# Spreading a column of maxima to all partitions: one turn of a repeated column in place of ones times a diagonal

## The reference

```python
xn = _layernorm(x)
# graph attention, twice (4 heads of 512, then 1 head of 768)
e = leaky_relu(al_s[src] + al_d[dst], 0.2)
m = segment_max(e, dst)              # one maximum for each node and head
ex = exp(e - m[dst])
alpha = ex / (segment_sum(ex, dst)[dst] + 1e-16)
out = segment_sum(h[src] * alpha, dst)
# keys of the linear attention, 12 heads, 256 features
data_dash = einsum('bhnd,md->bhnm', 64 ** -0.25 * k, proj)
m = max(data_dash)                   # ONE maximum over all nodes, heads and features
k_prime = ratio * (exp(data_dash - diag - m) + EPS)
context = einsum('bhnm,bhnd->bhmd', k_prime, v)
x = x + gnn(xn) + mix(xn)
x = x + ffn(layernorm(x))            # 8 experts, 2 chosen
```

## Time and profile before

| | us |
|---|---|
| median of 3 runs | 3684.7 (3683.17 to 3692.01) |
| the profiled execution, its own time | 3687.61 |
| its span, first to last instruction | 3685.8 |
| TensorE busy (matmul) | 3164.4, 86% |
| VectorE busy | 1971.2, 53% |
| GpSimd busy | 1508.9, 41% |
| mean granted TensorE clock | 0.919 of full speed |

### The profile page before, as it was taken

How to read it: one execution, slowest core, us unless ns; L and a number is a source line. 1 busy time by engine, 2 the same in 40 slices (tenths; PEclk the granted TensorE clock), 3 DMA queues, 4 the chain that set the end, 5 groups by cost and what they waited for, 6 DMA issues and landing times. The chain is left out here.

```text
span 3685.8 us, 64870 instructions
## 1 busy us (share of the span) xinstructions
PE 3164.4 (86%) x22058; PEld 2568.9 (70%) x22059; DVE 1971.2 (53%) x4639; ACT 1122.5 (30%) x2437; POOL 1508.9 (41%) x1496
## 2 busy tenths in 40 slices
PE   5994899999999689999799997799999996689920
PEld 4983677777777468888699997566666663479920
DVE  6753566676666454444422221566666664533357
ACT  1322344444444243333311111333333322223321
POOL 1233677777777300000000000777777761233346
PEclk8997999999999789999899998799999996589965
DMA  5655788888888354444465663999999984557767
GB/s 179 206 175 182 237 267 257 275 259 261 263 267 269 116 179 130 142 142 139 149 79 78 78 78 61 356 327 325 329 332 327 328 302 146 193 173 244 240 224 248
DMA packets 264982, 789.34 MB, mean 214 GB/s; under 512 B 81006, under 2 KB 94033, under 8 KB 257142
## 3 DMA queue, kind: packets, MB, share of 16 engines
q0 software_dynamic: 96640, 416.68, 34.7%
q1 hardware_dynamic: 168054, 369.05, 33.7%
HBM read 679.35 MB, written 167.42 MB: 230 GB/s over the span
## 5 line engine op out<-in xcount | busy, mean ns | idle before, releaser
L923 POOL DMA_INDIRECT k_rows<-tab,k_pick x576 | 598.5, 1039 | 234.8 <-issue 162.1
L2130 POOL DMA_INDIRECT m_rows<-tab,m_e x500 | 491.5, 983 | 200.4 <-issue 134.7
L1383 PE MATMUL k_num<-k_rows,k_wt 128*32 128x384 f32 (+1 forms) x3200 | 282.6, 493 | 12.5 <-ACT k_wt L1015 12.5
L142 PE MATMUL g_prod<-g_w_hi,g_h_h 128*128 128x384 f32 x768 | 258.6, 337 | 0.0
L1559 DVE TENSOR_TENSOR f_a_l<-f_turn,f_a_h 128x384 fp32r<-128x384 f32 x200 | 110.2, 552 | 277.4 <-ACT f_a_h L1531 277.2
L144 PE MATMUL g_prod<-g_w_hi,g_h_l 128*128 128x384 f32 x768 | 256.8, 334 | 0.0
L143 PE MATMUL g_prod<-g_w_lo,g_h_h 128*128 128x384 f32 x768 | 256.6, 334 | 0.0
L142 PE MATMUL f_prod<-f_w_hi,f_a_h 128*128 128x512 f32 x576 | 234.2, 407 | 0.0
L1685 POOL MEMSET g_row<- 128x1 f32 x2 | 0.1, 102 | 561.9 <-POOLq L109 561.9
L144 PE MATMUL f_prod<-f_w_hi,f_a_l 128*128 128x512 f32 x576 | 226.1, 393 | 0.0
L143 PE MATMUL f_prod<-f_w_lo,f_a_h 128*128 128x512 f32 x576 | 224.5, 390 | 0.0
(11 more groups left out here) (366 smaller groups left out, 7820.6 us busy)
## 6 DMA issues: line engine op xcount, KB each, us to landing
agg<-k_outb SPq DMA_DIRECT2D x100, 384.0 KB
f_a_in<-agg SPq DMA_DIRECT2D x100, 384.0 KB, 6.6
h<-f_e SPq DMA_DIRECT2D x25, 1024.0 KB, 4.2
g_h<-h SPq DMA_DIRECT2D x25, 1024.0 KB, 12.2
ys<-e_y SPq DMA_DIRECT2D x56, 384.0 KB, 3.0
tab<-q_xn SPq DMA_DIRECT2D x25, 388.5 KB, 5.9
tab<-g_row SPq DMA_DIRECT2D x25, 385.5 KB, 4.7
m_own<-tab SPq DMA_DIRECT2D x25, 385.5 KB, 9.1
```

Of the source, the lines that this page charges most:

```text
L142: pe.matmul(out, x_hi[k], w_hi[k], start=(k == 0), stop=False)
L923: pool.indirect_dma_start(rows[:, place(u, n), :], None, dram["tab1"], at, bounds_check=bound, oob_is_err=False).then_inc(rows_in[i], 16)
L1383: mm = pe.matmul(num[i][o, 0:n], wt[u % 2][:, v, o], rows[:, place(u, 2 * (half + v) + g), a:a + n], start=(v == 0), stop=(v == 1), tile_p ...
L2130: pool.indirect_dma_start(rows[:, place(h, c) + k, :], None, tab, bass.IndirectOffsetOnAxis(ap=e[h % 4][:, 0, k * SLOTS + c:k * SLOTS + c ...
```

## The change

The column on each partition is no longer put on a diagonal. TensorE's turn (a matmul in transpose mode with the identity) reads the one column 128 times over, with a step of zero along the free dimension: a 128 by 128 tile whose columns are all equal, and whose turn has in each row the whole column. This is done for mcol and rmax in K and for m2 in M. The instructions that made dg and dgm go, with their tiles and semaphores; in M the ones and their memset go too (K keeps ones for another product at its end). The waits of TensorE move from the diagonal to the column, and DVE waits for the spread of the set before ahead of overwriting the column, which it did ahead of overwriting the diagonal. The declarations of tiles and semaphores are left out here.

```diff
@@ -1085,16 +1085,12 @@
 
                 def row_max(t):
                     if t:
-                        dve.wait_ge(dgm_done, t)
+                        dve.wait_ge(top_full, t)
                     dve.tensor_reduce(rmax[:, :], r[:, :], AX.X, ALU.max).then_inc(rmax_done, 1)
-                    dve.wait_ge(rmax_done, t + 1)
-                    if t:
-                        dve.wait_ge(top_full, t)
                     if t == NT - 1:
+                        dve.wait_ge(rmax_done, t + 1)
                         dve.wait_ge(c_in, 16 * (3 if merged else 1))
                         dve.tensor_tensor(rmax[:, :], rmax[:, :], pad[:, :], ALU.add).then_inc(rmax_done, 1)
-                        dve.wait_ge(rmax_done, t + 2)
-                    dve.tensor_scalar(dgm[:, :], keep["ident"][:, :], rmax[:, 0:1], None, ALU.mult).then_inc(dgm_done, 1)
 
                 def running_max(t):
                     dve.wait_ge(top_full, t + 1)
@@ -1211,12 +1207,8 @@
                 def column_max(u):
                     dve.wait_ge(zt_full, u + 1)
                     if u:
-                        dve.wait_ge(dg_done, u)
+                        dve.wait_ge(mrow_full, u)
                     dve.tensor_reduce(mcol[:, :], zbank[:, 0:P], AX.X, ALU.max).then_inc(mcol_done, 1)
-                    dve.wait_ge(mcol_done, u + 1)
-                    if u:
-                        dve.wait_ge(mrow_full, u)
-                    dve.tensor_scalar(dg[:, :], keep["ident"][:, :], mcol[:, 0:1], None, ALU.mult).then_inc(dg_done, 1)
 
                 def shift(u):
                     dve.wait_ge(mrow_full, u + 1)
@@ -1340,12 +1332,12 @@
                     mm.then_inc(cx_full, 1)
 
                 def spread_max(t):
-                    pe.wait_ge(dgm_done, t + 1)
+                    pe.wait_ge(rmax_done, t + 1 if t < NT - 1 else t + 2)
                     if t:
                         pe.wait_ge(acc_done, 4 * t)
                     if merged:
                         pe.wait_ge(pick_done, min(t + 3, NT) if t else 2)
-                    pe.matmul(cx[:, 0:P], ones[:, :], dgm[:, :], start=True, stop=True).then_inc(top_full, 1)
+                    pe.transpose(cx[:, 0:P], rmax[:, 0:1].to_broadcast([P, P]), keep["ident"][:, :]).then_inc(top_full, 1)
 
                 def index_turns(t):
                     pe.wait_ge(ef_done, t + 1)
@@ -1368,8 +1360,8 @@
                     pe.transpose(zbank[:, 0:P], zmax[:, :], keep["ident"][:, :]).then_inc(zt_full, 1)
 
                 def edge_spread(u):
-                    pe.wait_ge(dg_done, u + 1)
-                    pe.matmul(zbank[:, P:2 * P], ones[:, :], dg[:, :], start=True, stop=True).then_inc(mrow_full, 1)
+                    pe.wait_ge(mcol_done, u + 1)
+                    pe.transpose(zbank[:, P:2 * P], mcol[:, 0:1].to_broadcast([P, P]), keep["ident"][:, :]).then_inc(mrow_full, 1)
 
                 def edge_sums(u):
                     pe.wait_ge(wt_done, u + 1)
...
@@ -2113,9 +2105,6 @@
         def _(pool):
             with pool.If(mine(pool)):
                 pool.memset(eps[:, :], MIX_EPS).then_inc(eps_set, 1)
-                if merged:
-                    pool.memset(ones[:, :], 1.0).then_inc(ones_set, 1)
-
                 def gathers(h):
                     pool.wait_ge(e_in[h % 4], 16 * GR * (h // 4 + 1))
                     pool.sem_inc(gather_go, 1)
@@ -2307,12 +2296,9 @@
                     dve.wait_ge(mcol_done, h + 1)
                     dve.wait_ge(zself_done, h + 1)
                     if h:
-                        dve.wait_ge(dg_done, h)
+                        dve.wait_ge(mrow_full, h)
                     dve.tensor_tensor(m2[:, :], mcol[:, :], zself[:, :], ALU.max).then_inc(m2_done, 1)
                     dve.wait_ge(m2_done, h + 1)
-                    if h:
-                        dve.wait_ge(mrow_full, h)
-                    dve.tensor_scalar(dg[:, :], keep["ident"][:, :], m2[:, 0:1], None, ALU.mult).then_inc(dg_done, 1)
                     if h:
                         dve.wait_ge(wself_done, h)
                     dve.tensor_tensor(dself[:, :], zself[:, :], m2[:, :], ALU.subtract).then_inc(dself_done, 1)
@@ -2439,8 +2425,8 @@
                     pe.transpose(zbank[:, 0:P], zmax[:, :], keep["ident"][:, :]).then_inc(zt_full, 1)
 
                 def edge_spread(h):
-                    pe.wait_ge(dg_done, h + 1)
-                    pe.matmul(zbank[:, P:2 * P], ones[:, :], dg[:, :], start=True, stop=True).then_inc(mrow_full, 1)
+                    pe.wait_ge(m2_done, h + 1)
+                    pe.transpose(zbank[:, P:2 * P], m2[:, 0:1].to_broadcast([P, P]), keep["ident"][:, :]).then_inc(mrow_full, 1)
 
                 def edge_sums(h, c):
                     if c == 0:
@@ -2455,8 +2441,6 @@
                     mm.then_inc(slot_done, 1)
 
                 pe.wait_ge(pj_in, 32)
-                if merged:
-                    pe.wait_ge(ones_set, 1)
                 for g in (0, 2, 4):
                     dashes(0, g)
                 for t in range(NT + 1):
```

More of the change, by code:

```diff
@@ L758, in mix_keys @@
         dsum, kd = s.sb("dsum", [P, HEADS]), s.sb2("kd", [P, HEADS])
-        rmax, dgm, top = s.sb("rmax", [P, 1]), s.sb("dgm", [P, P]), s.sb("top", [P, 1])
+        rmax, top = s.sb("rmax", [P, 1]), s.sb("top", [P, 1])
         run, neg, alpha = s.sb2("run", [P, 1]), s.sb("neg", [P, 1]), s.sb2("alpha", [P, 1])
@@ L765, in mix_keys @@
         (ones_set, acc_set, vsum_set, run_set, gemm_full, kc_done, vc_done, kt_full, kth_done, ktl_done, sq_done, dsum_done, kd_done,
-         dash_full, mx_done, nr_done, exp_done, rmax_done, dgm_done, top_full, top_done, run_done, neg_done, rd_done, sc_done,
+         dash_full, mx_done, nr_done, exp_done, rmax_done, top_full, top_done, run_done, neg_done, rd_done, sc_done,
          alpha_done, vs_done, vsum_done, cx_full, acc_done, eps_full, eps_done) = (s.sem(n) for n in (
              "ones_set", "acc_set", "vsum_set", "run_set", "gemm_full", "kc_done", "vc_done", "kt_full", "kth_done", "ktl_done",
-             "sq_done", "dsum_done", "kd_done", "dash_full", "mx_done", "nr_done", "exp_done", "rmax_done", "dgm_done",
+             "sq_done", "dsum_done", "kd_done", "dash_full", "mx_done", "nr_done", "exp_done", "rmax_done",
              "top_full", "top_done", "run_done", "neg_done", "rd_done", "sc_done", "alpha_done", "vs_done", "vsum_done",
@@ L779, in mix_keys @@
             wt, zmax = s.sb2("wt", [P, 2, P]), s.sb("zmax", [P, P])
-            mcol, dg, den, rden = s.sb("mcol", [P, 1]), s.sb("dg", [P, P]), s.sb("den", [P, 1]), s.sb("rden", [P, 1])
+            mcol, den, rden = s.sb("mcol", [P, 1]), s.sb("den", [P, 1]), s.sb("rden", [P, 1])
             outb = s.sb("outb", [P, D])
@@ L784, in mix_keys @@
             (gather_go, ef_done, ids_full, rel_done, cen_done, sqr_done, far_done, pick_done, other_done, pen_done, z1_part,
-             z2_done, z3_done, zmax_done, zt_full, mcol_done, dg_done, mrow_full, shift_done, wt_done, num_full, den_done,
+             z2_done, z3_done, zmax_done, zt_full, mcol_done, mrow_full, shift_done, wt_done, num_full, den_done,
              rden_done, out_done) = (s.sem(n) for n in (
                  "gather_go", "ef_done", "ids_full", "rel_done", "cen_done", "sqr_done", "far_done", "pick_done", "other_done",
-                 "pen_done", "z1_part", "z2_done", "z3_done", "zmax_done", "zt_full", "mcol_done", "dg_done", "mrow_full",
+                 "pen_done", "z1_part", "z2_done", "z3_done", "zmax_done", "zt_full", "mcol_done", "mrow_full",
                  "shift_done", "wt_done", "num_full", "den_done", "rden_done", "out_done"))
@@ L2014, in mix_out @@
         if merged:
-            ramp, ones = s.sb("ramp", [P, P]), s.sb("ones", [P, P])
+            ramp = s.sb("ramp", [P, P])
             e = [s.sb(f"e{b}", [P, 2, S], I32) for b in range(4)]
@@ L2020, in mix_out @@
             wt = s.sb2("wt", [P, SLOTS, GR, TW])
-            zmax, dg = s.sb("zmax", [P, P]), s.sb("dg", [P, P])
+            zmax = s.sb("zmax", [P, P])
             mcol, zs, zself, m2, dself, den, rden = (s.sb(n, [P, 1]) for n in ("mcol", "zs", "zself", "m2", "dself", "den", "rden"))
@@ L2028, in mix_out @@
             ald_in, own_in, rows_in = s.sem2("ald_in"), s.sem2("own_in"), keep["rows_in"][1]
-            (ones_set, gather_go, rel_done, other_done, z1_done, z2_done, z3_done, zmax_done, zt_full, mcol_done, zs_done,
-             zself_done, m2_done, dg_done, dself_done, mrow_full, shift_done, wself_done, wt_done, slot_done, acc_done,
+            (gather_go, rel_done, other_done, z1_done, z2_done, z3_done, zmax_done, zt_full, mcol_done, zs_done,
+             zself_done, m2_done, dself_done, mrow_full, shift_done, wself_done, wt_done, slot_done, acc_done,
              den_done, rden_done, out_done) = (s.sem(n) for n in (
-                 "ones_set", "gather_go", "rel_done", "other_done", "z1_done", "z2_done", "z3_done", "zmax_done", "zt_full",
```

(3 more changed lines are left out.)

## The result

The changed kernel takes 3663.73 us (median of 4 runs, 3662.95 to 3666.88), the kernel before 3686.8 us beside it. The ratio is 0.9945 [0.9933, 0.9956], so it is faster by 0.55%, some 20 us (the two medians lie 23.1 us apart; the interval covers both). A later group of runs on one chip gave 3668.66 us (3664.96 to 3671.73, 5 runs) against 3685.45, ratio 0.9951 [0.9938, 0.9964]. The forecast was 3669 and 15.4 us less. In the two profiled executions the difference is 3687.61 - 3664.49 = 23.1 us.

A forecast was written before the change was run, and what follows sets the result against it. TensorE was taken to bound K and drive the gathers. 0.15 + 0.08 + 0.42 = 0.65 us a tile over 23 tiles, 15.0 us, plus 0.4 in the last, made 15.4: 3684.7 - 15.4 = 3669 us, range 3661 to 3682.

The forecast's parts named there:

- (a): K, spread before a product in quarters 2 and 3: 0.24 us becomes 0.17, gain 0.15 us a tile for two.
- (b): K, spread before `contexts` in quarter 1: 0.33 us now, 0.08 us less.
- (c): K, keys' spread through quarter 0's spread to `contexts`: 4.68 us becomes 4.26 on TensorE's and DVE's paths, gain 0.42 a tile.
- low end of (c): K, keys' spread to `contexts`: gain only 0.34 us a tile if quarter 0's turn costs 0.26 us.
- (e): What shorter K meets next: gathers stay ahead, nothing new queues behind DVE, TensorE's waits are on earlier semaphores.
- (d): K's gains together: 0.65 us a tile, 15.0 us over 23 full tiles, some 0.4 us in the last tile.
- high ends: K's 23 full tiles with every gain at its upper bound: 20.7 us in all.
- (f): M, one spread a tile becomes a turn, hidden by the wait for DVE's residual: 0 us, 2 us if it counted.
- 1: Rival, K: the turn costs what the pair costs, leaving 8.5 us gain, 3676 us; chance 0.20.
- 2: Rival, K: the repeated column read is slow, load 0.56 us, kernel slower by 28 us, 3712; chance 0.05.
- 3: Rival, K: TensorE's clock drops for one set in a tile, 64 us less the gain, 3734; chance 0.03.
- 4: Rival: the change works but is all hidden or lost in scatter, time stays at 3684; chance 0.04.

The follow-up runs named there:

- Experiment 2: Kernel before with only TensorE's line changed to the turn, diagonals still made and waited for; 3667.85 us against 3682.44, ratio 0.9956.
- experiment 1: Changed kernel with an ordinary two-pass matmul in place of each turn, no diagonal; 3674.83 us against 3682.44 for the kernel before, ratio 0.9974.
- experiment 3: Kernel before with only the keys' running maximum in K spread by a turn, edges as before; 3681.4 us, ratio 0.9991.
- third run: Another profiled execution of the unaltered changed kernel, the slowest of its five; 3671.73 us.
- Experiment 4: Kernel before with only the second layer (M, `mix_out`) taken from the changed kernel; 3680.85 us, ratio 0.9991.

## Why the prediction was right, and where its steps were not

The sign, the size and the place are as forecast: 18 to 20 us by the ratios against 15.4, in K's tiles, by TensorE's path. That the mean tile is 35.11 us against the forecast 35.1 is partly luck: two terms were mis-sized in opposite directions.

**(a) and (b), mis-sized.** The steps gave 0.07 and 0.08 us each; measured are 0.24 - 0.08 = 0.16 and 0.33 - 0.16 = 0.17, so 0.49 us a tile instead of 0.23, and (a) lies beyond its own upper bound of 0.13. The fault is the row chosen. I set a turn ahead of L2406 (0.17) against a pair ahead of L142 (0.24). What a spread costs from start to start depends on what follows: the pair costs 0.24 ahead of L142 and 0.33 ahead of `contexts`, and the turn 0.08 and 0.16. The 0.09 between the successors was in the earlier trace rows, in the same view as the term. Against the same successor the difference is 0.16 to 0.17 in both places. Experiment 2 shows it with the diagonal kept.

**(c), right in the tiles with early rows, but by two errors, and too large on the mean.** It said 4.26 us from the keys' spread to `contexts`; such a tile has 4.28. On TensorE's path it got there as 4.68 - 0.23 - 0.11 - 0.08. The 0.11 was not gained (below), and the spread of quarter 0 gave 0.17 instead of 0.08: 4.68 - 0.23 - 0.17 = 4.28. That the two cancel is luck; that the diagonal's wait of 0.23 goes is the part that experiment 1 bears out. The low end of (c) is also lower than its own rows make it: with a turn at 0.26 ahead of `contexts` the spread still gains 0.07, as in (b), so it should have been 0.41, not 0.34. But what is left of the mean tile's 0.74 after (a) and (b) is 0.74 - 0.49 = 0.25 instead of 0.42; of the median tile's 0.88 it is 0.39. Two waits took the rest, both of which (e) denied. The keys' spread's own 0.11 us came back at once in `k_turns`, which now waits 0.23 us for ACT's copy of the values: from the keys' spread to the edges' turn it is 1.19 us, as before. And where rows are late, the edge maxima, and so DVE's whole chain down to the scaled values, are late too, and `contexts` comes after 4.60 or 4.92 us. Experiment 1 shows that DVE's part of (c) is real and comes from the diagonals, experiment 3 that the keys' own part in a median tile is not more than 0.11.

**(d)** gave 0.65 us a tile and 15.0 us; it is 0.74 and 17.0, two errors that partly cancel. The last tile brought 0.8 us instead of 0.4, and 1.3 us, no more than the scatter there, came ahead of the first spread, where I had the gathers hide it. The high ends made 20.7 us.

**(e)** is the step that failed in kind. I read 5 waits for rows as room. Before and after GpSimd does wait for TensorE (55.3 and 51.6 us), and still some sets come late, more of them now. They do not come late by chance. GpSimd starts a gather every 1.30 us (1.00 busy, 0.30 to the next), so its 24 gathers and its sum of the values take 24 x 1.30 + 1.70 = 32.9 us of a tile of 35. All 13 late sets of the changed kernel between 400 and 1200 us come 14.5 to 16.7 us after that sum started, 16 of 17 in its third run, 4 of the 5 before; and ahead of 11 of the 13 GpSimd had not waited for TensorE for over 18 us. For the wait of 1.08 us at 740.54 the sum is this:

```profile
725.20 1.70 POOL L932 TENSOR_TENSOR k_vsum<-k_vsum,k_v 128x768 f32<-128x768 f32 x1
```

So GpSimd's waits were an average over the tile that hid a stretch behind the sum in which it has no slack. That the sum is the cause is still argued, not shown: the kernel without it, meant to test it, met no ordinary execution.

**(f), M at 0**, held: the earlier trace rows showed the wait for the residual, and the projection still starts 0.57 us after the spread. Experiment 4, M changed alone, shows no gain either.

**The rivals.** 1: the turn does not cost what the pair costs; it costs a third ahead of a product (0.08 against 0.24) and half ahead of `contexts` (0.16 against 0.33). 2: the repeated read has a load of 133 ns where L1360's is 139; 0.56 us is refuted. The argument against this rival, that only the count of columns sets a load's time, was wrong as well: 128 columns take 188 ns in the pair and 140 in L1368's turn in the same, and the same repeated column 187 ns in an ordinary matmul (experiment 1). 3: the clock is 1.00 in K with 125 turns more in it than before. The Trainium skill (TensorE: Matmul & The Clock Gate, Part 4: PE-mode transpose) says that a transpose isn't counted as busy in the way a matmul is; at this share of turns, four spreads and the keys' in a tile beside the ten that were there, no row shows a cost of it. 4: nothing hid it.

## What to carry to other kernels

Where TensorE sets the time, price an instruction by the distance from its start to the start of the very instruction that will follow it, and compare old and new ahead of the same successor; two successors differed here by as much as the gain that was forecast. To bring a column from the partitions to all of them in fp32, one turn of the column read with a step of zero is cheaper than ones times a diagonal on both engines: in K it saved 0.16 us of TensorE's path and a DVE instruction of 0.32 us each time. A gain made in front of a cross-engine chain should be followed into the next two waits, and the order behind it reviewed: two calls moved gave another 9 us. And slack read from an engine's total of waits should be read again at the place in the tile where that engine has most to do.

## What the hardware showed that I had not expected

- The fp32 matmul by ones is two records and costs 0.16 us more than the turn ahead of the same successor (0.11 more ahead of turns: 0.22 against 0.11). Its load is also longer: 184 to 190 ns against 133 to 140, with the same operand (experiment 1).
- In M the same turn's load takes 192 ns in the median, not 133, while that of the turn of different columns there takes 138. No experiment separates the cause.
- Ahead of each edge spread, TensorE's load side idles 0.63 us with the diagonal or without it: behind the 32 matmuls in column groups the spread's load is not made ahead. It isn't all lost time, for the matmul side works meanwhile: the 32 end at 812.90 + 2.80 = 815.70, and the spread starts at 815.63. What a spread moved elsewhere in the queue would gain wasn't tried.
- In two groups of executions the same kernels take 4.13 to 4.16 ms, with stops of TensorE of about 1 us that the profile ascribes to nothing. The second of them has the chip number of a group at 3.66 to 3.69 ms. The changed kernel's ratio there, 0.997 [0.9953, 0.9988], can't be told from 0.9945 and 0.9951; but its profile can't be used to say what limits a tile otherwise.
